# Eight nested copies of the attention chunk in place of a loop over eight chunk bits, on three engines

## The reference, cut to what matters

```python
def _L0_xattn_ref(x, context, mask, W_q, W_k, W_v, W_o, b_o):
    q = (x @ W_q).reshape(b, n, HEADS, DIM_HEAD)
    k = (context @ W_k).reshape(b, j, HEADS, DIM_HEAD)
    v = (context @ W_v).reshape(b, j, HEADS, DIM_HEAD)
    sim = jnp.einsum('bihd,bjhd->bhij', q, k) * scale
    sim = jnp.where(mask[:, None, None, :], sim, max_neg)
    attn = jax.nn.softmax(sim, axis=-1)
    out = jnp.einsum('bhij,bjhd->bihd', attn, v).reshape(b, n, INNER)
    return out @ W_o + b_o
```

```python
_lenS2 = 2048 - jax.random.randint(jax.random.fold_in(_rk, 8), (8,), 0, max(1, 2048 // 4) + 1, jnp.int32)
_validS2 = jnp.arange(2048)[None, :] < _lenS2[:, None]
mask_BxS2_bk0 = jnp.logical_not(jnp.broadcast_to(_validS2[:, :], (8, 2048)))
```

## Time and profile before

| | |
|---|---|
| median of 3 runs | 781.46 us (776.91 to 785.27) |
| the profiled execution, its own time | 780.1 us |
| its span from first to last instruction | 778.4 us |
| TensorE busy | 665.1 us, 85% of the span |
| VectorE, ScalarE, GpSimd busy | 442.5, 356.1, 109.7 us |
| mean granted TensorE clock | 0.947 |
| first scores of the batch loop, last scores | 68.6 us, 381.5 us |

### The profile page before, as it was taken

How to read it: one execution, slowest core, us unless ns; L and a number is a source line. 1 busy time by engine, 2 the same in 40 slices (tenths; PEclk the granted TensorE clock), 3 DMA queues, 4 the chain that set the end, 5 groups by cost and what they waited for, 6 DMA issues and landing times.

```text
span 778.4 us, 14709 instructions
## 1 busy us (share of the span) xinstructions
PE 665.1 (85%) x4244; PEld 519.8 (67%) x4244; DVE 442.5 (57%) x960; ACT 356.1 (46%) x846; POOL 109.7 (14%) x143
## 2 busy tenths in 40 slices
PE   2896597969969696978969989999999899889996
PEld 1675486858858585867858867777777678634553
DVE  6822344444545444554475766666666534699974
ACT  2233233424434233433441136666666534468984
POOL 2581000010010101010020002222222100012211
PEclk9998888988989987998989999999999999999999
DMA  8000000000000000000545774444453243000111
GB/s 311 23 22 22 2 21 21 22 2 22 22 20 22 2 21 22 22 2 20 190 167 193 272 274 163 163 163 163 163 163 136 109 163 118 6 1 15 27 25 42
DMA packets 40064, 64.86 MB, mean 83 GB/s; under 512 B 4056, under 2 KB 20440, under 8 KB 40032
## 3 DMA queue, kind: packets, MB, share of 16 engines
q1 hardware_dynamic: 40032, 64.45, 24.3%
HBM read 53.95 MB, written 10.49 MB: 83 GB/s over the span
## 4 chain that ended last, share of the span: by engine, by line
PE 64%; DVE 13%; issue 11%; DMA 4%; DVEq 3%; ACT 2%; POOL 1%; SPq 0%; ACTq 0%; POOLq 0%
PE bank L570 33%; PE bank L699 6%; PE bank L930 5%; PE bank L687 3%; DMA absw<-in_L_ffn_w_down_dram 3%; PE bank L672 3%; PE bank L938 2%; PE bank L845 2%; PE bank L589 2%; DVE asum L1584 2%; DVE tern L1634 2%; DVE xn_a L1353 1%; PE bank L822 1%; PE bank L880 1%; PE bank L833 1%
## 5 line engine op out<-in xcount | busy, mean ns | idle before, releaser
L1049 ACT ACTIVATE probs<-probs,negm 128x256 f32<-128x256 f32 x104 | 52.1, 501 | 109.0 <-DVE negm L1450 109.0
L1450 DVE CUSTOM_DVE_ANT_0 probs<-bank,bias,negm_old 128x256 f32<-128x256 f32 x104 | 46.0, 480 | 64.2 <-PE bank L672 62.1
L672 PE MATMUL bank<-kT_hi,qT_hi 64*128 64x256 f32 x104 | 23.2, 440 | 51.6 <-issue 47.8
L930 PE MATMUL bank<-w_T,xqT 128*128 128x512 bf16 x256 | 58.4, 379 | 4.6 <-ACT xqT L1231 2.0
L467 POOL TENSOR_TENSOR rstd<-var_eps,neg_half 128x1 f32 (+1 forms) x16 | 10.0, 623 | 329.6 <-DVE var_eps L1513 260.3
L699 PEld LDWEIGHTS bank<-v_sb,pT 128*128 128x128 f32 x416 | 52.3, 191 | 5.5
L699 PE MATMUL bank<-v_sb,pT 128*128 128x64 f32 x416 | 54.7, 274 | 0.0
L1342 DVE TENSOR_TENSOR kT_lo<-bank,kT_hi 128x512 fp32r<-128x512 f32 x28 | 19.4, 692 | 58.2 <-ACT kT_hi L1038 58.2
L672 PEld LDWEIGHTS bank<-kT_hi,qT_hi 64*128 64x128 f32 x104 | 11.3, 214 | 61.3 <-issue 49.9
L1042 ACT COPY v_sb<-bank 128x512 f32<-128x512 f32 x28 | 15.1, 590 | 76.5 <-PE bank L699 73.5
L930 PEld LDWEIGHTS bank<-w_T,xqT 128*128 128x128 bf16 x256 | 24.1, 98 | 34.7 <-issue 2.9
(11 more groups left out here) (236 smaller groups left out, 1691.5 us busy)
## 6 DMA issues: line engine op xcount, KB each, us to landing
tern_dram<-tern SPq DMA_DIRECT2D x8, 768.0 KB, 5.2
tstage<-tern_dram SPq DMA_DIRECT2D x8, 768.0 KB, 4.3
cx<-in_ctx_dram SPq DMA_DIRECT2D x14, 384.0 KB, 2.9
absw<-in_L_ffn_w_gate_dram SPq DMA_DIRECT2D x8, 512.0 KB, 3.7
absw<-in_L_ffn_w_up_dram SPq DMA_DIRECT2D x8, 512.0 KB, 5.3
absw<-in_L_ffn_w_down_dram SPq DMA_DIRECT2D x8, 512.0 KB, 6.8
tern_raw<-in_L_ffn_w_gate_dram SPq DMA_DIRECT2D x8, 512.0 KB, 6.3
tern_raw<-in_L_ffn_w_up_dram SPq DMA_DIRECT2D x8, 512.0 KB, 7.2
```

The costliest lines, as they stand in the source:

```text
L672: last = mm(bank[3 + j][:, 0:CHUNK], part(qT, a)[o:o + DH, g, :], part(kT, c)[o:o + DH, g, :], start=(a == c), stop=(a == "lo"))
L930: last = mm(bank[3 + 2 * which + c % 2][:], xqT[:, u, k * P:(k + 1) * P], w_T[:, which, k, c * 512:c * 512 + 512], start=(k == 0), stop=(k ...
L1049: fn(probs[:, h, :], probs[:, h, :], ACT.Exp, bias=negm[:, h:h + 1], scale=-1.0, accum_out=csum[:, h:h + 1]).then_inc(p_done, 1)
L1450: nc.vector.tensor_tensor_reduce(probs[:, h, :], bank[3 + h % 2][:, 0:CHUNK], bias[:], -SCALE, negm_old[:, h:h + 1], ALU.add, ALU.min, neg ...
```

## The change

On TensorE, ScalarE and VectorE the loop over the eight bits of a batch goes. `each_live` takes the batch's eight bits into a register `left` and shifts them out of the word at once. Then it tests whether `left` is 0; if not, it clears the lowest set bit, runs a body, and inside that test makes the same test again, eight levels deep. So an engine runs one body for each live chunk and leaves the nest by one jump. The body stands eight times in the program of each of the three engines, where it stood once. SyncE and GpSimd are as before.

```diff
+        def each_live(eng, words, flag, body):
+
+            left = eng.alloc_register("chunks_left")
+            eng.reg_alu(left, words[0], (1 << NC) - 1, ALU.bitwise_and)
+            eng.reg_alu(words[0], words[0], NC, ALU.logical_shift_right)
+
+            def nest(depth):
+                with eng.If_ne(left, 0):
+                    eng.reg_alu(flag, left, 1, ALU.subtract)
+                    eng.reg_alu(left, left, flag, ALU.bitwise_and)
+                    body()
+                    if depth > 1:
+                        nest(depth - 1)
+
+            nest(NC)
...
             with pe.Fori(0, B) as b:
-                with pe.Fori(0, NC // UNROLL) as c:
-                    for u in range(UNROLL):
-                        with live(pe, words[0], flag):
-                            chunk(b, pe.snap(done))
-                            pe.reg_add(done, done, 1)
+                def live_chunk():
+                    chunk(b, pe.snap(done))
+                    pe.reg_add(done, done, 1)
+
+                each_live(pe, words, flag, live_chunk)
                 next_batch(pe, words, flag)
```

More of the change, by code:

```diff
@@ L1104, in _, with live_chunk @@
             with act.Fori(0, B) as b:
[L1105 to L1109, removed]
+                def live_chunk():
+                    chunk(b, act.snap(done))
+                    act.reg_add(done, done, 1)
+                each_live(act, words, flag, live_chunk)
                 next_batch(act, words, flag)
@@ L1534, in _, with live_chunk @@
             with dve.Fori(0, B) as b:
[L1535 to L1539, removed]
+                def live_chunk():
+                    chunk(b, dve.snap(done))
+                    dve.reg_add(done, done, 1)
+                each_live(dve, words, flag, live_chunk)
                 next_batch(dve, words, flag)
```

## The result

The change makes the kernel about 1.5% slower, a small loss but clear of the scatter: 791.44 us (788.93 to 795.59, six runs) against 780.91 us (776.91 to 785.27, six runs), a ratio of 1.0156 with a 95% interval of 1.0122 to 1.0189; every run of the change is above every run of before. The forecast of 785.7 us was 5.7 us too low. The profiled execution took 795.29 us, so 15.2 us over that of before; it lies 3.9 us above its own median, so sums made in it come out a few microseconds high.

What follows compares the result with a forecast made beforehand. Prediction: the walk over skipped bits bounds the kernel ahead of the scores; 780.1 - 40.8 saved + 45 for 15 instruction waits = 784.3 us profiled, 1.4 under the median, so 785.7 us; range 762 to 806.

Steps and rivals of the forecast that it cites:

- two waits of VectorE a batch: VectorE's jumps to the tail and back each wait 3.0 us for instructions; 15 waits add 45 us.
- the walk: Testing 51 skipped bits, 0.94 us each on TensorE, 0.78 on VectorE, is on the path; removing it saves 40.8 us.
- a second missing piece: Rival: past a jump's target the next instruction piece is missing too, 2.2 us more per boundary, 801 us; chance 0.27.
- first entry, with its first chunk: Before the first batch TensorE walks seven bits, 6.6 us, and keeps one test of 0.9: 5.7 us saved.
- seven boundaries (saved, two waits each): Between batches: savings of 6.2, 5.4 and five times 4.7 us, against two 3.0 us instruction waits each; net +6.9.
- last exit: The last batch's jump out to the tail waits 3.0 us for instructions, with no way back.
- dozens of transfers in the batch loop: Expected profile sign: dozens more instruction transfers between 64 and 400 us, on both queues.
- The first rival, that all is held: Engines keep the pieces used, so only one 3.0 us wait in the first batch: 743.7 us; chance 0.14.
- Who else pays: TensorE and ScalarE wait in parallel with VectorE, adding nothing; some 3 us of issue remains before TensorE's scores.
- the one on the clock: In a batch's first chunk, a higher clock behind a shorter pause gives back about 0.1 us a batch, left out.
- all of the tail moves by 3.0: VectorE's wait at its exit delays `on_c`, which TensorE's `turn_output` waits for, so the whole tail shifts 3.0 us.

Runs made afterwards that it cites:

- count_loop: Kernel before, with the bits counted once ahead of the batches and one body run per live chunk, no skipped bits or copied bodies: 741.74 us, ratio 0.9476.
- nest_of_2: The change with two nested bodies instead of eight, wrong for batches with more than two live chunks (none here): 739.17 us, ratio 0.9458.
- change_busy: The change plus unused identity transposes on TensorE, 14 behind `turn_context` in a batch's first chunk and 12 ahead of `turn_output`: 782.43 us, ratio 1.0021.
- gap_128_vector: Kernel before, with 128 never-executed VectorE instructions between chunk loop and tail, jumped over once a batch: 789.62 us, ratio 1.0108.

## Why the forecast was right, and where it was off

The forecast was right in its path and nearly in its sum: two waits of VectorE a batch eat what the walk gives back. The measured 791.4 us lie above the forecast by itself (785.7) and over the 789.3 to which it gave 0.34, nearly all of it for a second missing piece. That rival did not occur; other terms, which the forecast had at nothing, brought the time there.

The forecast had +4.2 us in terms of the profiled execution; that came out at +15.2. Both go into the same terms. A boundary goes from the start of the last `o_all` of a batch to the first maxima of the next, and a chunk from its first maxima to its last `o_all`; the seven boundaries add up to 80.8 us before and 92.4 after.

```
term                                    forecast   measured
first entry, with its first chunk         -5.7       -5.3
seven boundaries (saved, two waits each)  +6.9      +11.6
first chunks of the later batches          0         +5.4
between the two chunks of a batch, 5 x     0         -1.9
last exit                                 +3.0       +2.7
what follows the batch loop                0         +2.6
sum                                       +4.2      +15.1
```

**The walk saved what was forecast.** 40.8 us were to be saved; with one or two bodies `count_loop` saves 39.3 and `nest_of_2` 41.9. At the boundaries the working holds to the tenth: 34.9 us saved in `count_loop`, 35.1 forecast. That the total fits as well is in part luck. The first entry with its chunk gave 8.9 us there and not 5.7, the way from a batch's first chunk to its second 1.5 and not nothing, and the first chunks of the later batches took 6.0 back.

**The two waits came, near the forecast's price.** VectorE's sequencer stands for 2.7 us behind each of the two jumps at the fourth boundary, against 0.2 us behind a branch in the kernel before; the forecast took 3.0. VectorE's idle time, which has the tests behind the jump in it, is 2.7 us on the way out and 3.1 to 3.5 on the way back. With what hangs on them the eight bodies cost more than the waits: 45.6 us at the seven boundaries against `nest_of_2` (92.4 to 46.8; 42 forecast), and 52.3 in all against 45. The view that should show it, dozens of transfers in the batch loop, shows 49 from 64 to 412 us where none had been. The first rival, that all is held, holds for TensorE after the third batch and for ScalarE after the second, but not for VectorE, and one engine is enough. The rival of a second missing piece did not occur on VectorE in the change: its waits are single, and the second piece of each pair comes while it works.

**Who else pays** was told wrongly in part. Dozens of transfers were expected on both queues, with some 3 us of "issue" ahead of TensorE's scores in every batch; TensorE fetches in the first three batches only, and at the fourth boundary that pause is 0.34 us. It made little difference to the sum, save at the third boundary, where TensorE stands twice for 2.1 us ahead of `turn_output`: 15.4 us, 1.7 more than the one behind it.

**The step that failed** is the one on the clock: "a higher clock behind a shorter pause gives back about 0.1 us a batch, which I leave out". It had the sign wrong and the size. Without the walk the first chunks get longer, not shorter: 133.4 us in the change against 128.0, and 134.0 in `count_loop` and 131.9 in `nest_of_2`, which have no waits. So this part comes with the missing walk and not with the waits. In the kernel before, the long pause lies ahead of the scores, and scores and context are done while the clock is low. Without the walk they come at once, TensorE then stands until VectorE is there, and the clock is low under the keys and values. The waits add to this in the tail: TensorE stands ahead of `turn_output`, and each of its two groups of transposes takes 0.45 us longer (the first lies beside `xn_c`). `change_busy` takes 9.0 us of the clock's cost back.

The 0.1 us was read from the two stretches of the earlier trace rows. They are called the second batch's there, but the second batch has one live chunk; they are the third's. From first maxima to last `o_all` these two chunks take 17.6 us each, so this batch does not show the effect at all, while five other first chunks of the same kernel take 18.8, 18.1, 18.9, 18.9 and 18.1. One batch was too few to read it from.

**What was missed** is `xn_c`: "all of the tail moves by 3.0" moves VectorE's steps and not GpSimd's, and the two then overlap. By `gap_128_vector` that is 0.65 us of VectorE's tail, without a fetch and with transposes of 0.66 us; the second group of transposes at the lower clock adds 0.45, and the two make the 1.1. `change_busy` bears this out: with the transposes back at 0.66 us and `xn_c` still at 1.46, its tail takes 6.14 us, as in `gap_128_vector`.

**The first entry** came out at -5.3 against -5.7, but not for the reason given. The profiled execution of the change is 2.3 us later than that of before already ahead of the batch loop (`kT_lo`, 56.72 to 59.00), which no run explains; behind that it gains 6.7 us to the first maxima and 0.9 in the first chunk. And the forecast had nothing for the way from a batch's first chunk to its second, where the walk's one test is shorter now: 1.12 us to 0.74, five times.

The 2.6 us behind the batch loop stand in the profile (the difference grows from 12.5 us at the last `on_c`, 393.3 to 405.8, to 15.1 at `kT`, 460.5 to 475.6) and no run was made for them. As the profiled execution lies 3.9 us above its median, they may be no more than that.

## What to carry to other kernels

Before a loop body is copied, count how much program lies between the two ends that a steady loop visits on each engine, and look for the instruction transfers inside the loop: here four bodies were free and six cost 51 us (one run each), and the engine that paid was VectorE, not TensorE with its longer bodies. A walk over flags is better replaced by a count and one body than by nested bodies. And where a pause cannot be removed, ask what lies behind it on TensorE: a pause ahead of small work was cheaper here than the same pause behind it, and a few idle transposes gave back 9 to 10 us in two kernels, less in a third.

## What the runs showed that was not expected

- Two engines keep their programs differently. TensorE fetches 16 KB at a time, and steps over 2304 unused instructions in each batch without fetching again (1.001). VectorE fetches 8 KB at a time, and steps over 128 freely (one transfer) and over 384 not (33 transfers, +69 us). Whether VectorE keeps one stretch of the program or the last few pieces stays open: 4 bodies against 6, and 128 against 384, fit either. What is measured is that in the change it fetches five pieces a batch and waits for two. What TensorE keeps is open too: in the change it fetches again in the first three batches, over the gap of 2304 instructions it does not.
- A jump of VectorE to what is not there holds its sequencer for 2.7 us (2.0 where a second piece is missing behind a first), about as long as the 32 KB load of `mask_row` from issue to landing.
- A `TENSOR_SCALAR` of VectorE over 128x512 took 0.55 us when it started 0.25 us ahead of GpSimd's `TENSOR_TENSOR` of the same size, and 1.45 when it started 0.09 us behind it. In the order of before it was the next step of VectorE, `qT_lo`, that took 1.75 us instead of 0.68, which TensorE did not wait for.
- 4.2 us without work on TensorE ahead of the keys and values made that chunk 19.7 us long; 5.7 us without work ahead of the first scores and a turned context left the chunk at the same place of the kernel before at 18.0. Over the seven later batches the mean is 19.6 us against 18.3.
